# Row maxima of self-attention sent as transfers of 4-byte pieces, and output products in four units instead of two

## The chip, the cores and the metric

The kernel runs on one core of a Trainium2 chip. The metric is the device time of one execution in microseconds. The median of three runs of the kernel before is 3796.76 us.

## The reference

Four blocks in a row work on x of shape (4, 1024, 256), with a condition vector and 77 context rows per batch. L0 is a mixture of experts with a gate, L1 and L2 are transformer blocks (self-attention, cross-attention with the context, MLP), L3 is a cross-attention. The change touches the two self-attentions, which are (L1, in short; L2 has an adaptive normalisation and a gate `g_sa` on the result):

```python
h = layernorm(x, ln1_g, ln1_b)
q, k, v = heads(h @ wq + bq), heads(h @ wk + bk), heads(h @ wv + bv)   # 16 heads of 16
scores = einsum("bqhd,bkhd->bhqk", q, k) / 4                           # 1024 x 1024 per head
x = x + einsum("bhqk,bkhd->bqhd", softmax(scores), v) @ wo + bo + t_sa
```

## The kernel before

After the experts (L0) the program goes four times, once per batch, through one list of steps, `PASS`, written by `pass_schedule`. Every engine walks through the same list and issues what of each step is its own, so the list sets the order on all engines. Modules follow each other in it: L1sa, L1ca, L1mlp, L2sa, L2ca, L2mlp, L3ca; a step's first name is its module.

In a self-attention the 1024 tokens are 8 blocks of 128; `n` is one half of the queries (512, four blocks `t`), `g` one of four groups of four heads. A block of work is a pair (g, n), 8 per module. The softmax's maximum of each query must be known before the exponentials, and goes into the products themselves: q and k of a pair of heads are stacked in the rows of `qs` and `ks`, and row MAXROW of `qs` holds minus the maximum, beside a row of ones in `ks`. So there are two kinds of score products:

- step `A` (g, n, t, j): queries of block t as weights, all keys moving, into two PSUM banks (`ps<-ks,qs` in the trace). VectorE takes the negated maximum of each half of the keys (line 1721, `mxh`).
- step `both` (g, n): VectorE takes the minimum of the halves for all 4 blocks and 4 heads, 128x16 (line 1730, `mx`).
- step `M` (g, n): TensorE transposes `mx` (line 1069) into 16 rows of 128, ScalarE copies them to `mrow` (line 1390), and SyncE sends four transfers, each of 4 rows of 512 bytes, to row MAXROW of `qs` (`stack_maxima`, line 635).
- step `S` (g, n, kt, j): keys of block kt as weights, 512 queries moving (`ps<-qs,ks`). The first of a block waits for its transfers (`maxima_stacked`). ScalarE takes the exponential (line 1406, `probs`).
- steps `PV` (and `PVh`, its first half where score products for maxima are left): probabilities times v (`ps<-probs,v`), summed over kt. `O` copies the sum, `OT` (line 1122) turns it back to tokens, VectorE divides by the sum of exponentials.
- step `aT` turns the result of a half once more, `o` (t2) multiplies two blocks of 128 tokens by `wo` (`ps<-slot,hT` with 256 columns), VectorE adds to x (line 1687, in L2sa after a product with the gate, line 1682) and takes the statistics of the next normalisation, GpSimd the root (line 1768), and `N` (n) normalises the four token blocks of a half (line 1456, `tok`) for the next module. `T` (n) transposes them (line 983).

`self_attention` writes the order: all A, `both` and M in the list `maxima`, the S and PV in `units` of one (g, n, kt); `more` takes from `maxima` so that about two A go with each unit, and they end some 12 units before the last. Block (g, n)'s maxima are taken while an earlier block's units run. `turn` holds `both` and M of a block that is done: `both` comes before the next block's first A, M after its fourth (after the first for block (0, 0)). Near the end, behind unit `end - 6` come the two `aT` of the first half of the tokens, then o(0), o(1) and N(0) of the module that follows, one unit apart. PSUM banks of these steps are given out by `shared`, which takes the one asked for longest ago: A takes (0, 1) or (2, 3), the others (4 to 6) while A are left, and all seven afterwards; bank 7 is PV's. `mx` and `mxh` have two buffers each, used in turn by the blocks.

Of the kernel before, what the change touches and what calls it, by code (L numbers as in the profile page):

```python
# [25 lines left out]
F32 = mybir.dt.float32  # L26
# [6 lines left out]
P = 128  # L33
# [3 lines left out]
HALF = 512  # L37
# [82 lines left out]
def pass_schedule():  # L120
# [9 lines left out]
    def put(tag, *which):  # L130
        steps.extend((tag,) + w for w in which)
# [10 lines left out]
    def self_attention(tag, follow):  # L142
        maxima, turn = [], []
        for g in range(GROUPS):
            for n in range(NH):
                scores = [("A", g, n, t, j) for t in range(TPH) for j in range(GH)]

                behind = 1 if (g, n) == (0, 1) else 4
                maxima += turn[:1] + scores[:behind] + turn[1:] + scores[behind:]
                turn = [("both", g, n), ("M", g, n)]  # L150
        maxima += turn

# [26 lines left out]
        for u in range(end + lag):  # L179
# [23 lines left out]
            if u == end - 6:  # L203
                put(tag, *[("aT", 0, c) for c in range(KC)])
            elif u in (end - 5, end - 4):
                put(tag, ("o", u - end + 5))
            elif u == end - 3:
                put(follow, ("N", 0))
# [82 lines left out]
PASS = pass_schedule()  # L291
HALVED = {k for k in PASS if k[1] == "PVh"}

# [53 lines left out]
def build(nc, T, M):  # L347
    ctx = ExitStack()
    with ctx:
# [220 lines left out]
        def _(sp):  # L570
# [33 lines left out]
            for it in M.passes("blocks"):  # L604
# [18 lines left out]
                def stack_maxima(tag):  # L623

                    for g, n in [(g, n) for g in range(GROUPS) for n in range(NH)] if KIND[tag] == "self" else [(0, 0), (0, 1)]:
                        z, w, _, step = maxima_of(tag, g, n)
                        sp.wait_ge(act_done, upto(act_done, (tag,) + step))
                        if KIND[tag] == "cross":
                            for e in range(2):
                                sp.dma_start(qs[stacked(e, MAXROW, MAXROW + 1), 2 * g:2 * g + w // 2, n * HALF:(n + 1) * HALF].bitcast(F32),  # L630
                                             mrow[e:w:2, z * HALF:(z + 1) * HALF]
                                             ).then_inc(maxima_stacked[g][n], M.add(maxima_stacked[g][n], (tag, e), LOADED))
                        else:
                            for j in range(GH):
                                sp.dma_start(qs[stacked(j % 2, MAXROW, MAXROW + 1), 2 * g + j // 2, n * HALF:(n + 1) * HALF].bitcast(F32),
                                             mrow[TPH * j:TPH * (j + 1), z * HALF:z * HALF + P]
                                             ).then_inc(maxima_stacked[g][n], M.add(maxima_stacked[g][n], (tag, j - GH + 2), LOADED))
# [34 lines left out]
        def _(pe):  # L672
# [238 lines left out]
            for it in M.passes("blocks"):  # L911
# [9 lines left out]
                for name in PASS:  # L921
# [135 lines left out]
                    elif kind == "M":  # L1057
# [4 lines left out]
                        pe.wait_ge(act_done, upto(act_done, *act_was))  # L1062
                        last = (tag, "A", GROUPS - 1, n, TPH - 1, 0) if cross else (tag, "both", g, n)
                        pe.wait_ge(dve_done, upto(dve_done, last, *dve_was))
# [67 lines left out]
                    elif kind == "up":  # L1132
# [9 lines left out]
                        for i, (w, h) in enumerate(products):  # L1142
                            ins = mm(ps[:, b, :], w, h, i == 0, i == len(products) - 1)
                    elif kind == "o":

                        t2 = step[1]
                        a, banks = small()
                        _, act_was, dve_was = take(name, dve=(tag, "x", t2), banks=banks)
                        if KIND[tag] == "mlp":
# [7 lines left out]
                        pe.wait_ge(dve_done, upto(dve_done, *dve_was))  # L1157
                        for i in range(2):
                            t = 2 * t2 + i
# [6 lines left out]
                            else:  # L1166
                                for k in range(KC):
                                    ins = mm(ps[:, a, i * D:(i + 1) * D], hT[:, k, t * P:(t + 1) * P], wo[:, k, :], k == 0, k == KC - 1)
                    ins.then_inc(mm_done, M.add(mm_done, name))


        @block.scalar
        def _(act):
# [143 lines left out]
            for it in M.passes("blocks"):  # L1317
# [3 lines left out]
                for name in PASS:  # L1321
# [61 lines left out]
                    elif kind == "M":  # L1383
                        g, n = step[1:]
                        z, w, _, _ = maxima_of(tag, g, n)
                        act.wait_ge(mm_done, upto(mm_done, name))
                        if not cross and NH * g + n >= 2:
                            act.wait_ge(maxima_stacked[g - 1][n], upto(maxima_stacked[g - 1][n], (tag, 1)))
                        k, m = (w, HALF) if cross else (TPH * GH, P)
# [47 lines left out]
        def _(dve):  # L1437
# [198 lines left out]
            for it in M.passes("blocks"):  # L1636
# [4 lines left out]
                for name in PASS:  # L1641
# [81 lines left out]
                    elif kind == "both":  # L1723

                        g, n = step[1:]
                        z = maxima_of(tag, g, n)[0]
                        if NH * g + n >= 2:
                            dve.wait_ge(mm_done, upto(mm_done, (tag, "M", g - 1, n)))
                        dve.wait_ge(dve_done, upto(dve_done, (tag, "A", g, n, TPH - 1, GH - 1)))
                        dve.tensor_tensor(mx[:, z, 0, :].rearrange("p (c e t) -> p t c e", t=TPH, e=2), mxh[:, z, :, :, 0, :], mxh[:, z, :, :, 1, :], ALU.min  # L1730
                                          ).then_inc(dve_done, M.add(dve_done, (tag, "both", g, n)))
                    elif kind == "O" and by_dve(*name):
# [178 lines left out]
```

## Time and profile before

| | |
|---|---|
| median of 3 runs | 3796.76 us (3792.34 to 3797.68) |
| the profiled execution's own time | 3797.3 us |
| its span, first to last instruction | 3795.5 us |
| TensorE (PE) busy | 91% of the span |
| VectorE (DVE) busy | 59% |
| ScalarE (ACT) busy | 61% |
| granted TensorE clock, mean | 0.961 of full |
| transfers `qs<-mrow` of self-attention | 256, 2 KB each |
| DMA packets | 73089 |

Times in the rows below are microseconds from the span's start; L635 is line 635 of the kernel. "Idle before" in square brackets is how long the engine stood before the instruction, and what ended that. Matmuls are pipelined, so the distance between the starts of two of them tells more than their length. PE has a second row of its own for weight loads (PEld); SPq is the queue of SyncE.

### The profile page before, as it was taken

How to read it: one execution, taken by the hardware profiler on the slowest of the kernel's cores; microseconds unless marked ns; L12 is line 12 of the kernel's file. 1: busy time of each engine (PE TensorE's matmuls, PEld its weight loads, DVE VectorE, ACT ScalarE, POOL GpSimd, SP SyncE). 2: the span in 40 equal slices, each digit the busy share in tenths (PEclk: the TensorE clock that was granted, in tenths of full speed). 3: DMA queues.
4: the chain of work that ended last, by engine and by line, in shares of the span. 5: the costliest groups of instructions: out<-in, count | busy, mean ns of one | idle time of the engine just before them, and what ended most of it. 6: DMA issues, size and time to landing. Idle time of an engine off the chain costs nothing.

```text
span 3795.5 us, 59346 instructions
## 1 busy us (share of the span) xinstructions
PE 3443.8 (91%) x22289; PEld 2023.6 (53%) x22289; DVE 2237.3 (59%) x3533; ACT 2316.6 (61%) x4047; POOL 830.5 (22%) x546
## 2 busy tenths in 40 slices
PE   8999998898999888998898889988998899899988
PEld 6777776434644564446435744465446443564465
DVE  3323324885386556953885559636955487549654
ACT  2333333786577645875786557765874578657764
POOL 0322323003400521024003410051014100340051
PEclk8989989999999999999999999999999999999999
DMA  5001002000000001001000010000000100000000
GB/s 173 7 29 34 6 31 89 1 13 24 27 2 1 13 15 53 2 24 38 2 2 13 12 56 2 24 24 16 2 13 12 56 1 13 24 27 2 7 18 13
DMA packets 73089, 87.17 MB, mean 23 GB/s; under 512 B 11823, under 2 KB 62578, under 8 KB 72694
## 3 DMA queue, kind: packets, MB, share of 16 engines
q1 hardware_dynamic: 47846, 63.23, 5.1%
q10 hardware_dynamic: 24976, 20.15, 1.7%
q8 instruction: 195, 3.19, 0.4%
q14 instruction: 72, 0.59, 0.1%
HBM read 72.49 MB, written 9.56 MB: 22 GB/s over the span
## 4 chain that ended last, share of the span: by engine, by line
PE 76%; DVE 13%; ACT 7%; issue 2%; POOL 1%; DMA 0%; SPq 0%; ACTq 0%; DVEq 0%; POOLq 0%
PE ps L677 71%; DVE mxh L1721 4%; ACT probs L1406 3%; PE ps L1122 3%; DVE ctxk L1670 2%; DVE ow L1746 1%; PE ps L983 1%; DVE tok L1456 1%; DVE x L1687 1%; DVE small L1440 1%; DVE mx L1718 1%; ACT qs L1373 1%; POOL hidl L1832 1%; POOL small L1768 1%; ACT ow L1412 1%
## 5 line engine op out<-in xcount | busy, mean ns | idle before, releaser
L1406 ACT ACTIVATE probs<-ps 128x512 f32<-128x512 f32 (+1 forms) x2176 | 1216.5, 638 | 290.3 <-PE ps L677 247.7
L1721 DVE TENSOR_REDUCE mxh<-ps 128x2 f32<-128x1024 f32 x1024 | 1212.7, 1220 | 155.8 <-PE ps L677 152.7
L677 PE MATMUL ps<-probs,v 128*32 128x256 f32 (+2 forms) x7616 | 727.9, 454 | 6.3 <-ACT probs L1406 6.3
L677 PE MATMUL ps<-ks,qs 64*128 64x512 f32 x2048 | 483.1, 480 | 63.7 <-DVE mxh L1721 45.3
L1768 POOL TENSOR_TENSOR small<-small 128x4 f32<-128x4 f32 x66 | 67.8, 1027 | 2012.8 <-DVE small L1450 2012.8
L677 PE MATMUL ps<-qs,ks 64*128 64x512 f32 x2048 | 455.6, 425 | 4.0 <-DVE mxh L1721 2.5
L677 PEld LDWEIGHTS ps<-ks,qs 64*128 64x128 f32 x2048 | 192.8, 183 | 424.8 <-issue 302.0
L677 PEld LDWEIGHTS ps<-qs,ks 64*128 64x128 f32 x2048 | 248.1, 186 | 184.1 <-ACT probs L1406 150.1
L677 PEld LDWEIGHTS ps<-probs,v 128*32 128x32 f32 (+1 forms) x7616 | 150.2, 108 | 275.8 <-ACT probs L1406 204.6
L677 PE MATMUL ps<-hT,slot 128*128 128x512 f32 x448 | 233.5, 654 | 21.8 <-issue 8.5
L1718 DVE TENSOR_REDUCE mx<-ps 128x4 f32<-128x312 f32 x384 | 166.2, 478 | 146.2 <-PE ps L677 142.8
L1373 ACT ACTIVATE qs<-ps,cols 128x512 fp32r<-128x512 f32 x288 | 180.2, 687 | 101.5 <-PE ps L677 101.0
L677 PE MATMUL ps<-slot,hT 128*128 128x256 f32 x896 | 217.2, 387 | 9.3 <-ACT hT L1417 9.3
L1798 POOL TENSOR_TENSOR hidl<-hid,hidh 128x512 fp32r<-128x512 f32 x96 | 125.6, 1311 | 357.1 <-ACT hid L1282 357.1
L1687 DVE TENSOR_TENSOR x<-x,ps 128x512 f32<-128x512 f32 x80 | 55.0, 687 | 237.6 <-PE ps L677 237.6
L677 PEld LDWEIGHTS ps<-slot,hT 128*128 128x128 f32 x896 | 163.4, 190 | 58.2 <-issue 23.8
L1279 ACT ACTIVATE hidh<-ps,cols 128x512 fp32r<-128x512 f32 x96 | 66.1, 688 | 162.6 <-PE ps L677 162.4
L1832 POOL TENSOR_TENSOR hidl<-hid,hidh 128x512 fp32r<-128x512 f32 x128 | 161.7, 1300 | 7.2 <-ACT hid L1424 5.8
L1850 POOL TENSOR_TENSOR ql<-whole,qh 128x512 fp32r<-128x512 f32 x80 | 101.8, 1273 | 279.5 <-ACT whole L1358 279.5
L1122 PE MATMUL ps<-ident,ow 128*128 128x128 f32 x640 | 101.8, 282 | 60.6 <-DVE ow L1746 31.7
L983 PE MATMUL ps<-ident,tok 128*128 128x128 f32 x448 | 77.1, 311 | 80.3 <-DVE tok L1456 62.3
L677 PEld LDWEIGHTS ps<-hT,slot 128*128 128x128 f32 x448 | 85.5, 206 | 116.5 <-issue 90.5
(221 smaller groups left out, 5919.2 us busy)
## 6 DMA issues: line engine op xcount, KB each, us to landing
slot<-in_L_w SPq DMA_DIRECT2D x8, 1024.0 KB, 10.0
slot<-in_L_fc_w SPq DMA_DIRECT2D x8, 1024.0 KB, 5.4
xin<-in_x ACTq DMA_DIRECT2D x5, 1024.0 KB, 6.1
x_after_block<-x ACTq DMA_DIRECT2D x20, 256.0 KB, 2.4
xin<-x_after_block SPq DMA_DIRECT2D x5, 1024.0 KB, 5.5
ew<-in_L_e_w SPq DMA_DIRECT2D x6, 768.0 KB, 14.3
x<-in_x ACTq DMA_DIRECT2D x4, 1024.0 KB, 6.9
qs<-mrow SPq DMA_DIRECT2D x256, 2.0 KB
```

The costliest lines, as they stand in the source:

```text
L677: return pe.matmul(out, lhsT, rhs, start=start, stop=stop)
L983: ins = pe.transpose(ps[:, b, i * P:(i + 1) * P], tok[:, t, c * P:(c + 1) * P], ident[:])
L1122: ins = pe.transpose(ps[:, a, i * P:(i + 1) * P], ow[:, o:o + P], ident[:])
L1373: ins = act.activation(qs[:, pair, n * HALF:(n + 1) * HALF], ps[:, b, :], ACT.Identity, bias=qs_rows)
L1406: ins = act.activation(dst, src, ACT.Exp, scale=SCALE)
L1687: dve.tensor_tensor(xx, xx, src, ALU.add).then_inc(dve_done, M.add(dve_done, (tag, "x", t2)))
L1718: dve.tensor_reduce(mx[:, z, t, j0:j0 + GH], ps[:, a, 0:GH * SP_].rearrange("p (j s) -> p j s", s=SP_), AX.X, ALU.max, negate=True).then_i ...
L1721: dve.tensor_reduce(mxh[:, z, t, j // 2, j % 2, :], ps[:, a:a + 2, :], AX.X, ALU.max, negate=True).then_inc(dve_done, M.add(dve_done, name))
L1768: pool.tensor_tensor(rstd[:, tt], ve[:, tt], nhalf[:, tt], ALU.pow).then_inc(pool_done, M.add(pool_done, (tag, "rstd", h)))
L1798: pool.tensor_tensor(hidl0[:, (E * n + e) % 2, m % 4, :], hid0[:, m % 4, :], hidh0[:, (E * n + e) % 2, m % 4, :].bitcast(F32), ALU.subtrac ...
L1832: pool.tensor_tensor(hidl[:, n, m, :], hid[:, n, m, :], hidh[:, n, m, :].bitcast(F32), ALU.subtract).then_inc(pool_done, M.add(pool_done, ...
L1850: pool.tensor_tensor(lo[:, c, part], whole[:, whole_of(name)[0], 0:kn], hi[:, c, part].bitcast(F32), ALU.subtract).then_inc(pool_done, M.a ...
```

## The change

Blocks other than (0, 0) have no step M any more. `both` is now a step of each 128 queries, (g, n, t), 128x4, and stands behind the first A of the next t. As soon as it is done SyncE sends, for each of the four heads, one column of `mx` (128 partitions of one number, 4 bytes each) to 128 numbers in row MAXROW of `qs`: 16 transfers per block instead of four. The wait of a block's first S is for all 16. Block (0, 0) keeps its transposition and its four transfers, behind the minimum of its last t.

The output products of the first half are cut: `oh` (t2) multiplies the first 128 tokens, `o` (t2) the second into the same bank. The four stand behind the units `end - 5` to `end - 2`, and N(0) of the next module behind `end - 1`, two units later than before.

```diff
     def self_attention(tag, follow):
-        maxima, turn = [], []
+        maxima, last = [], []
         for g in range(GROUPS):
             for n in range(NH):
-                scores = [("A", g, n, t, j) for t in range(TPH) for j in range(GH)]
-
-                behind = 1 if (g, n) == (0, 1) else 4
-                maxima += turn[:1] + scores[:behind] + turn[1:] + scores[behind:]
-                turn = [("both", g, n), ("M", g, n)]
-        maxima += turn
+                for t in range(TPH):
+                    maxima += [("A", g, n, t, 0)] + last + [("A", g, n, t, j) for j in range(1, GH)]
+                    last = [("both", g, n, t)]
+                if (g, n) == (0, 0):
+                    maxima += last
+                    last = [("M", g, n)]
+        maxima += last
...
-            elif u in (end - 5, end - 4):
-                put(tag, ("o", u - end + 5))
-            elif u == end - 3:
+            elif u in (end - 5, end - 3):
+                put(tag, ("oh", (u - end + 5) // 2))
+            elif u in (end - 4, end - 2):
+                put(tag, ("o", (u - end + 4) // 2))
+            elif u == end - 1:
                 put(follow, ("N", 0))
...
                         z, w, _, step = maxima_of(tag, g, n)
+                        if KIND[tag] == "self" and (g, n) != (0, 0):
+                            for t in range(TPH):
+                                sp.wait_ge(dve_done, upto(dve_done, (tag, "both", g, n, t)))
+                                at_column = n * HALF + t * P
+                                for j in range(GH):
+                                    sp.dma_start(qs[stacked(j % 2, MAXROW, MAXROW + 1), 2 * g + j // 2, at_column:at_column + P].bitcast(F32),
+                                                 mx[:, z, 0, TPH * j + t:TPH * j + t + 1]
+                                                 ).then_inc(maxima_stacked[g][n], M.add(maxima_stacked[g][n], (tag, j - GH + 2) if t == TPH - 1 else None, LOADED))
+                            continue
                         sp.wait_ge(act_done, upto(act_done, (tag,) + step))
...
-                        for i in range(2):
+                        for i in (0,) if kind == "oh" else (1,) if in_two else range(2):
                             t = 2 * t2 + i
...
                     elif kind == "both":
 
-                        g, n = step[1:]
+                        g, n, t = step[1:]
                         z = maxima_of(tag, g, n)[0]
-                        if NH * g + n >= 2:
-                            dve.wait_ge(mm_done, upto(mm_done, (tag, "M", g - 1, n)))
-                        dve.wait_ge(dve_done, upto(dve_done, (tag, "A", g, n, TPH - 1, GH - 1)))
-                        dve.tensor_tensor(mx[:, z, 0, :].rearrange("p (c e t) -> p t c e", t=TPH, e=2), mxh[:, z, :, :, 0, :], mxh[:, z, :, :, 1, :], ALU.min
-                                          ).then_inc(dve_done, M.add(dve_done, (tag, "both", g, n)))
+                        if (g, n) == (1, 0):
+                            dve.wait_ge(mm_done, upto(mm_done, (tag, "M", 0, 0)))
+                        elif NH * g + n > 2 and t == 0:
+                            dve.wait_ge(maxima_stacked[g - 1][n], upto(maxima_stacked[g - 1][n], (tag, 1)))
+                        dve.wait_ge(dve_done, upto(dve_done, (tag, "A", g, n, t, GH - 1)))
+                        dve.tensor_tensor(mx[:, z, 0, :].rearrange("p (c e t) -> p t c e", t=TPH, e=2)[:, t], mxh[:, z, t, :, 0, :], mxh[:, z, t, :, 1, :], ALU.min
+                                          ).then_inc(dve_done, M.add(dve_done, (tag, "both", g, n, t)))
```

ScalarE's wait in step M for the transfers of two blocks ago goes too, since `mrow` is written once per module.

VectorE in the steady stretch of L1sa, from one division by the sums (`rc`, `tok`) to the next, before:

```order
L1756 RECIPROCAL rc<-ps 128x16
L1758 TENSOR_TENSOR tok<-ps,rc 128x4x64
L1721 TENSOR_REDUCE mxh<-ps 128x2 x4
L1730 TENSOR_TENSOR mx<-mxh 128x4x4
L1721 TENSOR_REDUCE mxh<-ps 128x2 x12
L1756 RECIPROCAL rc<-ps 128x16
L1758 TENSOR_TENSOR tok<-ps,rc 128x4x64
```

and now:

```order
L1774 RECIPROCAL rc<-ps 128x16
L1776 TENSOR_TENSOR tok<-ps,rc 128x4x64
L1737 TENSOR_REDUCE mxh<-ps 128x2
L1748 TENSOR_TENSOR mx<-mxh 128x4
L1737 TENSOR_REDUCE mxh<-ps 128x2 x4
L1748 TENSOR_TENSOR mx<-mxh 128x4
L1737 TENSOR_REDUCE mxh<-ps 128x2 x4
L1748 TENSOR_TENSOR mx<-mxh 128x4
L1737 TENSOR_REDUCE mxh<-ps 128x2 x4
L1748 TENSOR_TENSOR mx<-mxh 128x4
L1737 TENSOR_REDUCE mxh<-ps 128x2 x3
L1774 RECIPROCAL rc<-ps 128x16
```

Sixteen reductions stand there in both; one minimum of 128x16 has become four of 128x4, each behind the first reduction of the following t.

TensorE in L1sa around the end of the maxima, where the last M stood, before:

```order
L677 MATMUL ps<-probs,v 32x256 x4
L677 MATMUL ps<-ks,qs 128x512 x2
L1069 MATMUL ps<-ident,mx 16x128
L677 MATMUL ps<-qs,ks 128x512 x2
L677 MATMUL ps<-probs,v 32x512 x4
```

and now:

```order
L689 MATMUL ps<-probs,v 32x256 x4
L689 MATMUL ps<-ks,qs 128x512 x2
L689 MATMUL ps<-qs,ks 128x512 x2
L689 MATMUL ps<-probs,v 32x512 x4
```

The score products for the exponentials follow the last one for the maxima directly.

TensorE in L1sa from o(0) (`slot_99,hT`) to the transposition T(0) of L1ca (`ident,tok`), before:

```order
L677 MATMUL ps<-slot_99,hT 128x256 x4
L677 MATMUL ps<-qs,ks 128x512 x2
L677 MATMUL ps<-probs,v 32x512 x4
L677 MATMUL ps<-qs,ks 128x512 x2
L677 MATMUL ps<-slot_99,hT 128x256 x4
L677 MATMUL ps<-qs,ks 128x512 x2
L677 MATMUL ps<-probs,v 32x512 x4
L677 MATMUL ps<-qs,ks 128x512 x4
L677 MATMUL ps<-probs,v 32x512 x4
L677 MATMUL ps<-qs,ks 128x512 x4
L677 MATMUL ps<-probs,v 32x512 x4
```

and now, from the first half of o(1) on:

```order
L689 MATMUL ps<-slot_99,hT 128x256 x2
L689 MATMUL ps<-qs,ks 128x512 x2
L689 MATMUL ps<-probs,v 32x512 x4
L689 MATMUL ps<-qs,ks 128x512 x2
L689 MATMUL ps<-slot_99,hT 128x256 x2
L689 MATMUL ps<-qs,ks 128x512 x2
L689 MATMUL ps<-probs,v 32x512 x4
L689 MATMUL ps<-qs,ks 128x512 x2
L689 MATMUL ps<-probs,v 32x512 x8
L995 MATMUL ps<-ident,tok 128x128 x8
```

Behind the last output product now stand one unit's PV and S, the last PV, and T(0) (`ident,tok`); before, the S of two more units stood between.

## Rows read from the trace of the kernel before

**Rows 1.** The page: busy time of the engines, and the chain that ended last.
```profile
PE 3443.8 (91%) x22289; PEld 2023.6 (53%) x22289; DVE 2237.3 (59%) x3533; ACT 2316.6 (61%) x4047; POOL 830.5 (22%) x546
...
PE 76%; DVE 13%; ACT 7%; issue 2%; POOL 1%; DMA 0%; SPq 0%; ACTq 0%; DVEq 0%; POOLq 0%
```

**Rows 2.** Timeline, TensorE, steady stretch: start, us, line, operation, [idle before <-ended by].
```profile
738.57 0.50 PE L677 MATMUL ps<-ks,qs 64*128 64x512 f32 x2
739.00 0.28 PE L1069 MATMUL ps<-ident,mx 128*16 128x128 f32 x1
...
740.24 0.50 PE L677 MATMUL ps<-ks,qs 64*128 64x512 f32 x2
740.57 0.40 PE L677 MATMUL ps<-qs,ks 64*128 64x512 f32 x2
...
741.47 0.50 PE L677 MATMUL ps<-ks,qs 64*128 64x512 f32 x2
...
750.04 0.66 PE L1122 MATMUL ps<-ident,ow 128*128 128x128 f32 x4 [0.43 <-ACT ow L1412]
...
771.45 0.66 PE L1122 MATMUL ps<-ident,ow 128*128 128x128 f32 x4 [0.43 <-ACT ow L1412]
```

**Rows 3.** Timeline, VectorE, the same stretch.
```profile
757.12 0.19 DVE L1730 TENSOR_TENSOR mx<-mxh 128x16 f32<-128x16 f32 x1
757.22 4.61 DVE L1721 TENSOR_REDUCE mxh<-ps 128x2 f32<-128x1024 f32 x4
```

**Rows 4.** Timeline, end of the maxima of the first L1sa.
```profile
840.64 0.50 PE L677 MATMUL ps<-ks,qs 64*128 64x512 f32 x2
842.72 0.19 DVE L1730 TENSOR_TENSOR mx<-mxh 128x16 f32<-128x16 f32 x1
...
843.06 0.27 PE L1069 MATMUL ps<-ident,mx 128*16 128x128 f32 x1 [1.92 <-DVE mx L1730]
...
843.25 0.52 PE L677 MATMUL ps<-qs,ks 64*128 64x512 f32 x2
...
849.67 0.73 PE L677 MATMUL ps<-qs,ks 64*128 64x512 f32 x4
```

**Rows 5.** Windows between two copies of the sum: us, busy by engine, granted clock, DMA.
```profile
834.98:872.97 37.99, 34.86 (x234) 13.14 (x233) 14.34 (x30) 29.27 (x59) 1.02 (x1) 1.00 0.09 29
...
2763.05:2803.61 40.56, 37.39 (x235) 13.56 (x233) 15.72 (x32) 29.37 (x60) 1.02 (x1) 0.92 0.01 1
...
sum 314.48, PE 289.28 PEld 106.96 DVE 120.25 ACT 234.33 POOL 8.14; mean PE 36.16 PEld 13.37 DVE 15.03 ACT 29.29 POOL 1.02
```

**Rows 6.** Timeline, VectorE, in the lead of the first L1sa.
```profile
679.88 9.23 DVE L1721 TENSOR_REDUCE mxh<-ps 128x2 f32<-128x1024 f32 x8 [0.34 <-PE ps L677]
```

**Rows 7.** Timeline, SyncE's queue and TensorE, block (0, 0)'s transfers.
```profile
690.08 2.54 SPq L635 DMA_DIRECT2D qs<-mrow  x4
...
693.71 0.57 PE L677 MATMUL ps<-qs,ks 64*128 64x512 f32 x2 [0.60 <-DMA qs<-mrow]
```

**Rows 8.** DMA issues: count, KB each, us from issue to landing.
```profile
ident<-in_ident SPq DMA_DIRECT2D x1, 64.0 KB, 2.3
```

**Rows 9.** One tile (`cond`): duration ns min/median/max, first and last start.
```profile
L1180 ACTq DMA_DIRECT2D cond<-in_condT x9: 486/487/700, 1.9 to 3011.3; - x9
```

**Rows 10.** Timeline, end of the first L1sa.
```profile
864.82 0.50 PE L677 MATMUL ps<-qs,ks 64*128 64x512 f32 x2
...
868.16 1.38 DVE L1456 TENSOR_SCALAR tok<-x,small 128x256 f32<-128x256 f32 x4 [1.13 <-POOL small L1768]
...
871.84 1.07 PE L677 MATMUL ps<-probs,v 128*32 128x512 f32 x8 [0.78 <-ACT probs L1406]
```

**Rows 11.** Timeline, end of the first L2sa.
```profile
1216.53 0.51 PE L677 MATMUL ps<-qs,ks 64*128 64x512 f32 x2
...
1217.36 0.69 DVE L1687 TENSOR_TENSOR x<-x,tok 128x512 f32<-128x512 f32 x1
...
1220.59 1.38 DVE L1456 TENSOR_SCALAR tok<-x,small 128x256 f32<-128x256 f32 x4 [1.13 <-POOL small L1768]
```

More of the change, by code:

```diff
@@ L291 @@
 PASS = pass_schedule()
-HALVED = {k for k in PASS if k[1] == "PVh"}
+HALVED = {k for k in PASS if k[1] in ("PVh", "oh")}
 def by_dve(tag, kind, *step):
@@ L1062, in _ @@
                         pe.wait_ge(act_done, upto(act_done, *act_was))
-                        last = (tag, "A", GROUPS - 1, n, TPH - 1, 0) if cross else (tag, "both", g, n)
+                        last = (tag, "A", GROUPS - 1, n, TPH - 1, 0) if cross else (tag, "both", g, n, TPH - 1)
                         pe.wait_ge(dve_done, upto(dve_done, last, *dve_was))
@@ L1143, in _ @@
                             ins = mm(ps[:, b, :], w, h, i == 0, i == len(products) - 1)
-                    elif kind == "o":
+                    elif kind in ("oh", "o"):
                         t2 = step[1]
-                        a, banks = small()
-                        _, act_was, dve_was = take(name, dve=(tag, "x", t2), banks=banks)
+                        in_two = (tag, "oh", t2) in HALVED
+                        if kind == "oh" or not in_two:
+                            a, banks = small()
+                            _, act_was, dve_was = take((tag, "o", t2), dve=(tag, "x", t2), banks=banks)
+                        else:
+                            a, act_was, dve_was = M.where(name), [], []
                         if KIND[tag] == "mlp":
@@ L1168, in _ @@
                                     ins = mm(ps[:, a, i * D:(i + 1) * D], hT[:, k, t * P:(t + 1) * P], wo[:, k, :], k == 0, k == KC - 1)
+                        if kind == "oh":
+                            continue
                     ins.then_inc(mm_done, M.add(mm_done, name))
@@ L1386, in _ @@
                         act.wait_ge(mm_done, upto(mm_done, name))
-                        if not cross and NH * g + n >= 2:
-                            act.wait_ge(maxima_stacked[g - 1][n], upto(maxima_stacked[g - 1][n], (tag, 1)))
                         k, m = (w, HALF) if cross else (TPH * GH, P)
```

## The prediction

> **What bounds the kernel now.** The page's totals and its chain of waits come first: TensorE is busy for 91% of the span and carries 76% of the chain that ended last [rows 1]. Half a microsecond won on TensorE is therefore won for the kernel wherever TensorE runs without a gap, and nothing is won beside it. The change touches the two self-attention modules (L1sa, L2sa), run for each of 4 batches: 8 passes.
>
> The timeline of TensorE in a steady stretch shows such a pass [rows 2]. Score products for the maxima (`ks,qs`, step A) start every 1.23 us (740.24 to 741.47) without idle time. Where the transposition of the maxima (step M, L1069) stands between two of them, the step is 1.67 us (738.57 to 740.24). From one output transposition to the next (750.04 to 771.45), one block of four heads and 512 queries, 21.41 us pass. VectorE is close behind but not the bound: with work waiting it makes four reductions in 4.61 us, so (4.61 - 1.22)/3 = 1.13 us each, against TensorE's 1.23 [rows 3]. The small minimum (`both`, L1730) lasts 0.19 us, but the next reduction starts 0.10 us after it [rows 3].
>
> At the end of the maxima the cost is another [rows 4]: after the last score product (840.64) TensorE idles 1.92 us for the last minimum before it can transpose, and its next product starts at 843.25, 2.61 us after the last A instead of the 0.33 us between 740.24 and 740.57 [rows 2]. In six of the eight passes more follows: the stretch that holds this idle time is 37.99 us long with the full clock, but up to 40.56 us with a granted clock of 0.92, that is, part of it at 1.2 GHz instead of 2.4; the eight stretches add up to 314.48 us [rows 5].
>
> **What the change removes.** Of 8 transpositions M per pass 7 go, with 7 ScalarE copies and 28 transfers. Six stand in the steady stretch: 1.67 - 1.23 = 0.44 us each, 6 x 8 x 0.44 = **21.1 us**. I take all of it, because TensorE has no gap there and neither VectorE (1.13 against 1.23) nor ScalarE waits behind it. The seventh stands at the end of the maxima: 2.61 - 0.33 = 2.28 us, times 8 = **18.2 us**. The S products that follow need nothing of VectorE. With the idle time the clock drop behind it should go too: 314.48 - 8 x 37.99 = **10.6 us**. Its bounds are 0 (the drops only move) and 10.6. I take 10.6, since two passes with the same idle time and no drop bear out what the stretch takes at full clock.
>
> **What it adds on VectorE.** 32 minima of 128x4 instead of 8 of 128x16 per pass, 24 more. Each costs the queue 0.10 us by the start of the reduction behind it [rows 3]; the bounds are 0 and the whole 0.19 us. In the steady stretch TensorE's 1.23 leaves 0.10 us per reduction, 0.40 us per four, for one minimum: hidden. The minimum is queued behind the next reduction, whose end it need not wait for, and a second pair of banks holds the product meanwhile. In the lead it is not hidden: eight reductions from 679.88 follow each other in 9.23 us without a gap, so VectorE is the bound there [rows 6]. Two new minima fall into that run: 2 x 0.10 x 8 = **1.6 us lost** (0 to 3 x 0.19 x 8 = 4.6).
>
> **What it adds on SyncE and the DMA engines.** 16 transfers per block instead of 4, each of 128 pieces of 4 bytes: 7 x 16 - 28 = 84 more per pass. They hold up nobody but step S of their block, and behind them on SyncE stand only loads that wait for the end of the maxima anyway. Two prices are unknown, issue and landing. Issue: four of today's (4 pieces each) take 2.54 us, 0.64 each [rows 7], and a load of 128 pieces of 8 bytes takes 0.487 us [rows 9]. Landing: a load of 128 pieces of 512 bytes with little ahead of it lands 2.3 us after its issue [rows 8]; from the start of the fourth issue of today's (690.08 + 3 x 0.64 = 692.0) to TensorE's start at 693.71 are 1.7 us [rows 7]. So the last minimum of a block is followed by 3 x 0.64 + 2.3, and 0.1 to react, 4.3 us (lower bound 3 x 0.49 + 1.7 = 3.2). What is available: in the steady stretch S of a block follows 8 A products after the first of the next block, 7 x 1.23 + 0.33 = 8.9 us, less some 2.3 us (two reductions of 1.13) until VectorE has made the minimum: 6.6 us. At block (3,1) it is tighter: the minimum starts at 842.72 and lasts 0.19, the new minima ahead of it may push its end to 843.0, and S(3,1,0,0), the third of the four `qs,ks` products from 849.67, starts at about 850.0 and will start 2.28 us earlier: 847.7 - 843.0 = 4.7 us [rows 4]. **Cost 0**, with 0.4 us to spare there, which rival 2 weighs. Sixteen issues of 0.64 are 10.2 us of a block of 21; what dearer ones would do is rival 1.
>
> The rows of 128 pieces are loads from memory; none goes from 128 partitions into one. The Trainium skill (DMA: Bandwidth & Descriptors, Rules for kernel authors) speaks against the change: it says to coalesce many small transfers into a large one, and that a strided last dimension becomes one descriptor per element and should be rearranged. No row here shows such a transfer. By that rule the time would come out on the other side, which is the first rival below.
>
> **The output products.** Steps o(0) and o(1), 1.99 us each today, become four of half that in the next four units, and the normalisation N(0) moves from behind unit 61 to behind unit 63. TensorE's work is the same. Gained: today TensorE waits 0.78 us for the last exponentials [rows 10], because they were bunched behind the two long products; with four short ones I leave 0.15, so 0.63 gained per pass. Lost: the transposition T(0) of the next module comes sooner after the last output product. From the end of o(1) (864.82) TensorE has 0.43 + 1.00 + 0.42 + 1.00 + 1.00 + 0.15 = 4.0 us of work, and T(0)'s first four transpositions would be done at 4.5. The normalised rows are there at 868.16 + 1.38 - 864.82 = 4.72 us [rows 10], and the fourth transposition ends at about 4.9: 0.4 lost. In L2sa a product with the gate comes first: 1220.59 + 1.38 - 1216.53 = 5.44, so 1.1 lost [rows 11]. There the bank of o(0) is also wanted by an S product 1.43 us after it, while VectorE lets go of it at 1217.36 + 0.69 - 1216.53 = 1.52 [rows 11]: 0.15 more. Per pass +0.2 in L1sa and -0.65 in L2sa, together 4 x 0.45 = **1.8 us lost** (bounds: 8 x 0.63 = 5.0 gained, 4 x 3 = 12 lost if the wait costs the clock again).
>
> **The sum.** 21.1 + 18.2 + 10.6 - 1.6 - 1.8 = 46.5 us. The profiled execution took 3797.3 us (span 3795.5), 0.5 above the median of the three runs, 3796.8; against that median the forecast is 3796.8 - 46.5 = **3750.3 us**, 1.2% faster. This kernel can be told from no change at about 0.2%, 7.6 us.
>
> **The rivals.**
> 1. *SyncE and its small transfers become the bound* (slower). Place: step S of every block. Sixteen transfers must go out in the 21.0 us that a block lasts without its transposition, so it decides from 21.0/16 = 1.31 us per transfer, and the kernel as a whole is slower from about 1.37: 16 x 1.37 - 21.0 = 0.9 us per block, times 48 blocks, is 44 us. At 1.5 us it would be 3 x 48 = 144 us, 3894 us. For it: no row has 4-byte pieces into one partition. Against it: 0.487 us for the nearest piece count [rows 9]. Chance 0.07.
> 2. *The last block's transfers land late* (4.3 us grows past 4.7). At 6 us 1.3 us are lost in each pass, 10.4 in all: 3761 us. Chance 0.11.
> 3. *The clock gives nothing back*, because the drops move, or because L2sa's wait before T(0) brings one: 3750.3 + 10.6 = 3761 us, up to 3769 with drops of 2 us at four of them. Chance 0.12.
> 4. *VectorE takes over the steady stretch*: 24 x 8 x 0.19 = 36 us lost of 46.5, 3787 us. Against it is its 0.10 us of slack per reduction. Chance 0.03.
> 5. *The transpositions were hidden*, so that only o's shift is seen: 3797 us. The step of 1.67 us speaks against it. Chance 0.02.
>
> **How the numbers follow.** The forecast has 0.65. Its own range runs from 3741 (all gains, T(0) not waiting: 46.5 + 1.6 + 6.8 = 54.9 gained) to 3759 (minima at 4.6, so 3.0 more, and both waits before T(0) twice as long, so 4 x 1.5 = 6.0 more). Rivals 2 and 3 reach to 3769. The range 3740 to 3770 leaves out rivals 1, 4 and 5 and some of the tails, about 0.18. Faster by over 0.2%: 0.65 + 0.11 + 0.12 + 0.02 = 0.90; within 0.2%: 0.03; slower: 0.07.
>
> **What would show it.** Right: the step from one output transposition to the next falls from 21.41 to 21.0; TensorE no longer waits for the minimum at the end of the maxima; the eight stretches last about 35.1 us (37.99 - 2.28 - 0.63) with a clock of 1.00; packets grow by about 896 x 128 = 115,000; a TensorE wait of 0.4 us (L1sa) and 1.1 us (L2sa) stands before T(0). Wrong: waits of TensorE for `qs<-mx`, an issue over 1.3 us, a granted clock below 1 behind the wait for T(0), or TensorE waits for reductions in the steady stretch.

## The result, and the profile after

The changed kernel takes 3807.47 us (median of 13 runs, 3795.10 to 3816.78) against 3792.44 us for the kernel before, measured beside it; the ratio is 1.0044, 95% interval 1.0031 to 1.0058, without one of the 13 executions of the kernel before that took 6517.69 us. It is **slower by 0.44%, some 17 us**, where 46.5 us faster were forecast.

The profiled execution of the changed kernel (3795.1 us) is the fastest of its 13, and a plain comparison of the two spans (3793.3 against 3795.5 us) misleads. The self-attention's first score product stands at 649.30 us in it and at 665.67 before: 16.4 us won in the experts, whose code is untouched. In the profiles of this study that product stands at 649 to 652 us or at 660 to 666 us, with the changed maxima and without them: the experts vary between executions (why is not shown), and that variation is in every ratio below. So I compare the passes by stage, and for the experiments I also give the time from that first score product to the end of the span: 3129.8 us before, 3144.0 after, **14.2 us more**. First the page of the changed kernel:

```profile
PE 3426.3 (90%) x22233; PEld 2018.0 (53%) x22233; DVE 2286.4 (60%) x3725; ACT 2306.2 (61%) x3991; POOL 831.2 (22%) x546
...
PE 77%; DVE 13%; ACT 6%; issue 2%; POOL 1%; DMA 1%; SPq 0%; ACTq 0%; DVEq 0%; POOLq 0%
...
qs<-mx SPq DMA_DIRECT2D x896, 0.5 KB, 2.0
```

Against [rows 1] TensorE is busy 17.5 us less, yet the median time is not less. Windows show where the time goes. These are the eight leads, from the first score product to the first output transposition (columns: window, length, busy time of PE, PEld, DVE, ACT and POOL, granted clock, DMA share, GB/s). Before:

```profile
665.67:728.63 62.96, 55.16 (x328) 26.66 (x328) 51.40 (x47) 41.74 (x74) 8.36 (x4) 1.00 0.00 1
...
sum 504.91, PE 443.21 PEld 213.78 DVE 411.19 ACT 329.92 POOL 66.97; mean PE 55.40 PEld 26.72 DVE 51.40 ACT 41.24 POOL 8.37
```

And after:

```profile
649.30:718.91 69.61, 57.65 (x327) 28.31 (x327) 56.43 (x55) 41.57 (x73) 8.33 (x4) 0.95 0.03 1
...
sum 552.60, PE 458.50 PEld 224.49 DVE 451.71 ACT 328.16 POOL 66.65; mean PE 57.31 PEld 28.06 DVE 56.46 ACT 41.02 POOL 8.33
```

**The leads have grown by 47.7 us**, with VectorE busy 40.5 us longer and the granted clock at 0.95 in all eight. The steady stretches behind them (first to last output transposition but the tail's) sum, before and then after:

```profile
sum 856.27, PE 839.06 PEld 354.23 DVE 792.30 ACT 716.95 POOL 0.00; mean PE 104.88 PEld 44.28 DVE 99.04 ACT 89.62 POOL 0.00
```

```profile
sum 839.37, PE 822.50 PEld 349.65 DVE 794.15 ACT 706.28 POOL 0.00; mean PE 102.81 PEld 43.71 DVE 99.27 ACT 88.29 POOL 0.00
```

16.9 us less. The ends of the maxima, from the last score product for maxima to the step `aT`, before and then after:

```profile
2768.70:2786.87 18.17, 16.21 (x95) 4.75 (x91) 3.55 (x6) 13.08 (x28) 0.00 (x0) 0.81 0.01 1
...
sum 135.31, PE 119.83 PEld 36.51 DVE 28.32 ACT 103.91 POOL 0.00; mean PE 14.98 PEld 4.56 DVE 3.54 ACT 12.99 POOL 0.00
```

```profile
2764.10:2778.08 13.98, 13.64 (x94) 4.34 (x91) 3.59 (x6) 12.81 (x27) 0.00 (x0) 1.00 0.04 2
...
sum 111.84, PE 109.15 PEld 34.70 DVE 28.69 ACT 102.43 POOL 0.00; mean PE 13.64 PEld 4.34 DVE 3.59 ACT 12.80 POOL 0.00
```

23.5 us less, with the clock at 1.00 in all eight. What follows up to the output transposition behind T(0) is 8.5 us longer (148.80 against 140.27 us over the eight passes, from `aT`). Together: 47.7 - 16.9 - 23.5 + 8.5 = 15.8 us slower in the self-attentions, where the medians say 17 with an interval of 12 to 22.

The lead's growth has one place. VectorE in the changed kernel, first lead:

```profile
658.21 1.06 DVE L1748 TENSOR_TENSOR mx<-mxh 128x4 f32<-128x4 f32 x1
...
664.65 4.00 DVE L1748 TENSOR_TENSOR mx<-mxh 128x4 f32<-128x4 f32 x1
...
674.63 0.15 DVE L1748 TENSOR_TENSOR mx<-mxh 128x4 f32<-128x4 f32 x1
```

GpSimd in the same stretch:

```profile
657.97 1.28 POOL L1868 TENSOR_TENSOR ql<-whole,qh 128x512 fp32r<-128x512 f32 x1 [3.61 <-ACT whole L1376]
...
664.10 4.53 POOL L1841 TENSOR_TENSOR x<-xin,rows_now 128x2048 f32<-128x2048 f32 x1
```

And TensorE:

```profile
669.93 0.79 PE L689 MATMUL ps<-ks,qs 64*128 64x512 f32 x2 [4.55 <-DVE mxh L1737]
...
683.26 3.46 PE L689 MATMUL ps<-slot,hT 128*128 128x256 f32 x8
```

A minimum of 512 numbers lasts **4.00 us** where others last 0.15. It ends at 668.65 and GpSimd's addition at 668.63; the one of 1.06 us ends at 659.27 and GpSimd's subtraction at 659.25. The pattern repeats in all eight passes (1.06 to 1.07 and 3.99 to 4.01 us): 8 x (3.85 + 0.91) = 38 us of VectorE's 40.5. TensorE stands 4.55 us, and a stretch at half clock begins behind it (its next products of keys and queries last 0.79 us instead of 0.49). A second such stretch follows in the same lead, at 683.26, where eight products with `slot` last 3.46 us instead of the 1.99 of the kernel before. In the kernel before the lead's one minimum comes at 689.14, and GpSimd's addition is over by then, at 685.04:

```profile
680.47 4.57 POOL L1823 TENSOR_TENSOR x<-xin,rows_now 128x2048 f32<-128x2048 f32 x1
```

The Trainium skill (SBUF — State Buffer, Who interferes with whom) has the rule: a VectorE instruction with two inputs in SBUF and a GpSimd instruction that reads SBUF exclude each other, and whichever comes second waits until the first is done. This trace agrees to 0.02 us, twice in each pass. The reductions of PSUM in the lead, beside the same addition, keep their pace: 9.23/8 = 1.15 us [rows 6].

### The profile page after: what moved, and what is told of

Same layout as the page of the kernel before. It is cut to its first block, busy times and chain, and to the rows that moved or that the text cites. A ratio compares the mean times of both kernels' runs of the same rounds, so it can differ in the third digit from the quotient of the medians.

```text
span 3793.3 us, 59978 instructions
## 1 busy us (share of the span) xinstructions
PE 3426.3 (90%) x22233; PEld 2018.0 (53%) x22233; DVE 2286.4 (60%) x3725; ACT 2306.2 (61%) x3991; POOL 831.2 (22%) x546
## 2 busy tenths in 40 slices
DMA packets 200328, 87.28 MB, mean 23 GB/s; under 512 B 139951, under 2 KB 189810, under 8 KB 199926
## 4 chain that ended last, share of the span: by engine, by line
PE 77%; DVE 13%; ACT 6%; issue 2%; POOL 1%; DMA 1%; SPq 0%; ACTq 0%; DVEq 0%; POOLq 0%
PE ps L689 72%; DVE mxh L1737 3%; PE ps L1134 3%; ACT probs L1422 2%; DVE ctxk L1686 2%; DVE ow L1764 1%; PE ps L995 1%; DVE tok L1472 1%; DVE small L1456 1%; ACT qs L1391 1%; DVE x L1703 1%; DVE mx L1748 1%; POOL small L1786 1%; DVE mx L1734 1%; ACT ow L1428 1%
## 5 line engine op out<-in xcount | busy, mean ns | idle before, releaser
L689 PE MATMUL ps<-slot,hT 128*128 128x256 f32 x896 | 227.4, 397 | 9.3 <-ACT hT L1433 9.3
```

The source lines that it names most:

```text
L689: return pe.matmul(out, lhsT, rhs, start=start, stop=stop)
```

## The experiments

Ratios are to the kernel before, measured beside each group of experiments, with their 95% intervals; it took 3787 us beside e1 to e4, 3788 beside e5 to e8 and 3796 beside e9 and e10. "x us faster" is worked out from the ratio. The second figure for each leaves the experts out; it comes from one profiled execution each, from the first score product of self-attention to the end of the span, against the 3129.8 us of before:

| | by the ratio | first score product to end |
|---|---|---|
| e1 | 22 faster | 23.0 faster |
| e2 | 42 faster | 34.4 faster |
| e3 | 28 faster | 39.9 faster |
| e4 | 43 slower | 42.7 slower |
| e5 | 42 faster | 34.8 faster |
| e6 | 53 faster | 43.4 faster |
| e7 | 12 slower | 6.8 slower |
| e8 | 22 faster | 21.2 faster |
| e9 | 33 slower | 51.2 slower |
| e10 | 46 faster | 42.7 faster |

**e1: one minimum for block (0, 0).** Its result is not needed before its transposition, so cutting it buys nothing.

```diff
+                if (g, n) == (0, 1):
+                    last = [("both", 0, 0, TPH - 1), ("M", 0, 0)]
                 for t in range(TPH):
                     maxima += [("A", g, n, t, 0)] + last + [("A", g, n, t, j) for j in range(1, GH)]
-                    last = [("both", g, n, t)]
-                if (g, n) == (0, 0):
-                    maxima += last
-                    last = [("M", g, n)]
+                    last = [("both", g, n, t)] if (g, n) != (0, 0) else []
```

> The changed kernel, but block (0, 0), whose maxima are still transposed, keeps one minimum of 128x16 instead of four of 128x4. In the profile of the changed kernel the minimum of its second 128 queries lasts 4.00 us in each of the 8 passes, and ends with GpSimd's addition x<-xin (4.53 us) beside it; the first lasts 1.06 us. Theory A, a minimum with both inputs in SBUF waits while GpSimd works: the lead loses its 46.8 us over the 8 passes, about 3759 us (3752 to 3768), no minimum over 0.3 us. Rival B, each extra VectorE instruction in the lead costs only its own time: 3 x 8 x 0.15 = 4 us less than the change, about 3803 us. Rival C, the small transfers slow the kernel: no change, 3807 us.

Measured 3766.65 us, ratio 0.9942 (0.9920 to 0.9965). No minimum lasts over 0.3 us, B and C fall, but about 8 us of the expected gain are missing. I had put the minimum behind the next block's first score product, where the kernel before has it ahead; its transposition waits for that reduction too, 1.51 us instead of the 0.44 before, 8.6 us in eight passes:

```profile
674.14 0.27 PE L1080 MATMUL ps<-ident,mx 128*16 128x128 f32 x1 [1.51 <-DVE mx L1748]
```

Four of its eight leads also have a granted clock of 0.95 or 0.97.

**e2: the same four minima with one input.**

```diff
+                        if (g, n) == (0, 0):
+                            dve.tensor_reduce(mx[:, z, 0, :].rearrange("p (c e t) -> p t c e", t=TPH, e=2)[:, t], mxh[:, z, t].rearrange("p c h e -> p c e h"), AX.X, ALU.min
+                                              ).then_inc(dve_done, M.add(dve_done, (tag, "both", g, n, t)))
+                            continue
```

> The changed kernel with its four minima of block (0, 0) in the same places, each made by a TENSOR_REDUCE of the halves (one input) instead of a TENSOR_TENSOR of two. A: if two inputs in SBUF are what waits for GpSimd, these last about 0.15 us beside the addition, and the time is that of the kernel with one minimum plus up to 4 us, 3759 to 3763 us. Rival A2, any VectorE operation on SBUF waits for GpSimd: still 4 us at the second minimum, 3807 us. Rival B: 3807 us.

Measured 3744.71 us, ratio 0.9889 (0.9862 to 0.9915), 14 us below what I had said. Its four runs lie between 3737 and 3759 us, and the profiled one, whose trace I read, is the 3759. In that one the experts take 12 us more than in e1's profile (the first score product stands at 661.47 us against 649.22), and three leads have stretches at half clock; whether the others lack both is not on record. VectorE, then GpSimd:

```profile
670.38 0.15 DVE L1749 TENSOR_REDUCE mx<-mxh 128x4 f32<-128x8 f32 x1
...
676.83 0.15 DVE L1749 TENSOR_REDUCE mx<-mxh 128x4 f32<-128x8 f32 x1
```

```profile
676.28 4.58 POOL L1845 TENSOR_TENSOR x<-xin,rows_now 128x2048 f32<-128x2048 f32 x1
```

The same numbers from SBUF into SBUF, in the middle of the addition, in 0.15 us. A stands, A2 falls. The edit changes the operation together with the number of inputs; a row of the changed kernel tells the two apart, a TENSOR_TENSOR whose one input is in SBUF and the other in PSUM, inside a GpSimd subtraction:

```profile
867.97 1.27 POOL L1868 TENSOR_TENSOR ql<-whole,qh 128x512 fp32r<-128x512 f32 x1 [4.64 <-ACT whole L1376]
```

```profile
868.35 0.69 DVE L1703 TENSOR_TENSOR x<-x,ps 128x512 f32<-128x512 f32 x1 [1.94 <-PE ps L689]
```

It lasts 0.69 us, as it does with GpSimd idle (849.72), and all 80 of them last 0.68 to 0.69. So it is the second input in SBUF.

**e3: the addition later.**

```diff
+                        if KIND[tag] == "self":
+                            pool.wait_ge(dve_done, upto(dve_done, (tag, "both", 0, 0, TPH - 1)))
                         pool.tensor_tensor(x[:], ...
```

> The changed kernel with its four two-input minima, but GpSimd's addition x<-xin of the self-attention waits until the last minimum of block (0, 0). A: the second minimum falls from 4.00 to about 0.15 us; the first keeps its 1.06 us (GpSimd's kl<-whole,kh is still beside it); the time is about 3760 us (3754 to 3772), a few us more if the addition meets the minima of block (0, 1). Rival B or C: 3807 us.

Measured 3759.03 us, ratio 0.9926 (0.9900 to 0.9951). VectorE in the lead:

```profile
661.06 1.06 DVE L1748 TENSOR_TENSOR mx<-mxh 128x4 f32<-128x4 f32 x1
...
667.51 0.16 DVE L1748 TENSOR_TENSOR mx<-mxh 128x4 f32<-128x4 f32 x1
```

The second minimum is short again, the first still waits for GpSimd's subtraction of 1.27 us, as expected. So GpSimd's instruction matters, not the place in VectorE's order.

**e4: the kernel before with only that.** Block (0, 0)'s minimum cut into four; transpositions, transfers and output products as before.

```diff
+                if (g, n) == (0, 0):
+                    scores = [s for t in range(TPH) for s in [("A", g, n, t, 0)] + [("both", g, n, t - 1)] * (t > 0) + [("A", g, n, t, j) for j in range(1, GH)]]
```

> The kernel before with one part of the change alone: block (0, 0)'s minimum cut into four of 128x4, behind the first score product of the next 128 queries, as in the change; everything else (transpositions, transfers, output products) as before. A: the lead's loss is this and nothing else, so about 47 us slower than before, 3839 us (3830 to 3846). Rival B: 4 us slower, 3796 us. Rival C: as before, 3792 us.

Measured 3829.53 us, ratio 1.0114 (1.0090 to 1.0139), 43 us slower. Its leads, as windows:

```profile
649.18:719.95 70.77, 59.10 (x328) 29.05 (x329) 56.38 (x50) 41.71 (x74) 8.32 (x4) 0.93 0.00 1
...
sum 559.11, PE 466.88 PEld 226.28 DVE 450.89 ACT 329.91 POOL 66.55; mean PE 58.36 PEld 28.28 DVE 56.36 ACT 41.24 POOL 8.32
```

54.2 us more than before in the leads, with the clock at 0.93 to 0.95; the steady stretches and the ends of the maxima are as before, and it is 9 us less between the passes, where the granted clock of the longer stretches is 0.94 to 0.95 against 0.92 to 0.93. Three more small instructions per pass cost nearly as much as the whole change was to bring, 46.5 us.

**e5: e1 with the minimum in its old place.**

```diff
+                if (g, n) == (0, 1):
+                    maxima += [("both", 0, 0, TPH - 1)]
+                    last = [("M", 0, 0)]
```

> The changed kernel with one minimum of 128x16 for block (0, 0), this time ahead of the next block's first score product, where the kernel before has it. e1 had it behind that product, and its transposition M waited 1.51 us instead of 0.44 (8 x 1.07 = 8.6 us). Expected: M waits 0.44 us again, the lead is 0.3 us a pass shorter than in the kernel before, and the whole 38 to 43 us faster than before (3745 to 3752 us if before is 3788). If e1's remaining distance to e2 was something else, the time stays at e1's, 20 us below before.

Measured 3746.35 us, ratio 0.9888 (0.9862 to 0.9914), as expected. This is the change without its mistake: 42 us faster.

**e6: e5 with the output products in two units, as before.** The maxima alone are changed.

> As e5, and the output products of the first half in two units as in the kernel before, so the maxima alone are changed. By the prediction's own step the split costs 1.8 us over the 8 passes, so this would be 1.8 us faster than e5; if the shorter wait for the last exponentials is the larger part, it is up to 5 us slower; if the wait before T(0) counts more than I took, up to 12 us faster.

Measured **3738.14 us**, ratio 0.9861 (0.9839 to 0.9883): 53 us faster than before and the best of the study. It is 8.2 us below e5 in the medians and 8.6 us in the profiles without the experts, more than the step's 1.8. In the traces the stretches from `aT` to the output transposition behind T(0) sum to 148.80 us in e5 and 140.20 in e6. The rest of e6 has what the maxima give, as windows: the leads, and then the ends of the maxima:

```profile
sum 500.29, PE 438.09 PEld 212.95 DVE 412.34 ACT 327.90 POOL 66.98; mean PE 54.76 PEld 26.62 DVE 51.54 ACT 40.99 POOL 8.37
```

```profile
sum 111.88, PE 109.18 PEld 34.73 DVE 28.72 ACT 102.45 POOL 0.00; mean PE 13.65 PEld 4.34 DVE 3.59 ACT 12.81 POOL 0.00
```

**e7: the kernel before with the output products in four units.** The edit is the change's own for `oh` and `o`, with `N(0)` behind `end - 1`.

> The kernel before with the output products' part alone: first half in four units, N(0) behind the last unit. By the prediction 1.8 us slower than before, with the wait for the last exponentials down from 0.78 to 0.15 us and a wait before T(0); bounds 5 us faster and 12 us slower. In the changed kernel's trace the distance from the first product behind the maxima to T(0) in the first L1sa is 29.30 us against 29.13, so I look for about 2 to 6 us slower.

Measured 3803.79 us, ratio 1.0031 (1.0015 to 1.0048), 12 us slower; its trace has 8.5 us more from `aT` on (148.78 against 140.27 us): 0.54 in a pass of L1sa and 1.60 in one of L2sa. TensorE at the end of the first L2sa:

```profile
1215.64 0.59 PE L679 MATMUL ps<-qs,ks 64*128 64x512 f32 x2 [0.18 <-ACT probs L1414]
1216.15 1.13 PE L679 MATMUL ps<-slot,hT 128*128 128x256 f32 x4
...
1221.80 0.59 PE L679 MATMUL ps<-qs,ks 64*128 64x512 f32 x2 [0.17 <-ACT probs L1414]
1222.32 2.19 PE L679 MATMUL ps<-probs,v 128*32 128x512 f32 x16
1224.75 1.64 PE L985 MATMUL ps<-ident,tok 128*128 128x128 f32 x8 [0.24 <-DVE tok L1464]
1226.23 0.60 PE L1124 MATMUL ps<-ident,ow 128*128 128x128 f32 x4
```

The wait before T(0) is 0.24 us, less than I had taken. But from T(0)'s first transposition to the next step's pass 1.48 us where it was 0.93 (1224.55 to 1225.48 in the kernel before), because the normalised rows `tok` arrive one by one (VectorE writes the four from 1224.19 to 1225.57), and score products wait twice, 0.18 and 0.17 us, for a bank that ScalarE still reads. One half of an output product (the row of x4) costs 1.06 us from start to next start, more than half of the 1.92 of the whole (x8).

**e8: the kernel before with the new way for block (3, 1) alone.** Seven blocks keep their transposition.

> The kernel before with the new way for the last block (3, 1) alone: its four minima of 128x4 and 16 transfers of 4-byte pieces; the other seven blocks keep their transposition. This separates the idle time at the end of the maxima and the clock behind it from the steady stretch. Expected: the steady step stays 21.41 us, TensorE's wait of 1.92 us is gone, no granted clock below 1 between it and T(0) in any pass; 23 to 29 us faster than before. If the clock drops only move, 12 to 18 us.

Measured 3771.00 us, ratio 0.9943 (0.9921 to 0.9964), 22 us faster. Two of the stretches of [rows 5] in it, the second being the one that was 40.56 us long:

```profile
829.70:866.08 36.38, 34.82 (x235) 13.16 (x232) 14.38 (x31) 29.11 (x58) 1.02 (x1) 1.00 0.12 30
2740.73:2777.10 36.37, 34.81 (x235) 13.14 (x232) 15.77 (x33) 29.11 (x58) 1.02 (x1) 1.00 0.03 1
```

All eight sum to 291.01 us, 23.5 below the 314.48 of before: 1.6 us each for the idle time and 10.6 for the clock, and the drops do not come back before T(0).

**e9: twice as many small transfers.** As e5, each of 64 pieces instead of 128.

```diff
                                 for j in range(GH):
-                                    sp.dma_start(qs[stacked(j % 2, MAXROW, MAXROW + 1), 2 * g + j // 2, at_column:at_column + P].bitcast(F32),
...
+                                    for part in range(2):
+                                        sp.dma_start(qs[stacked(j % 2, MAXROW, MAXROW + 1), 2 * g + j // 2, at_column + 64 * part:at_column + 64 * part + 64].bitcast(F32),
+                                                     mx[64 * part:64 * part + 64, z, 0, TPH * j + t:TPH * j + t + 1]
...
```

> As e5, but each of the small transfers cut in two: 32 per block, of 64 pieces of 4 bytes, 1792 in all. It tells how far SyncE and the small transfers are from being the bound (rival 1). In the changed kernel's trace one issue takes 0.60 us in the median and lands in 2.0 us. If an issue's price does not depend on its number of pieces: 32 x 0.6 = 19.2 us of SyncE in a block of 21.0, so the steady stretch still holds at 21.0, but the last block's transfers come later than its first score products and TensorE waits there: up to 10 us slower than e5. If the price goes with the pieces (0.3 us each): as e5. If it is above 0.66 us with two per head: the blocks get longer, 1 us or more each, over 50 us.

Measured 3825.54 us, ratio 1.0086 (1.0063 to 1.0109), 33 us slower than before where e5 is 42 faster. SyncE's queue runs without a pause through the steady stretch, and TensorE waits for it at the end of the maxima:

```profile
715.97 84.34 SPq L636 DMA_DIRECT2D qs<-mx  x125
```

```profile
837.95 0.57 PE L690 MATMUL ps<-qs,ks 64*128 64x512 f32 x2 [2.86 <-DMA qs<-mx]
```

84.34/125 = 0.67 us per transfer of 64 pieces, and 32 of them, 21.6 us, do not fit into a block of 21.0: the third case of the expectation. An issue costs nearly the same with half the pieces (0.597 us in the median against 0.601), so with 16 transfers, 10.7 us at that rate, the change has nearly a factor of two in hand.

**e10: no transposition at all.** As e6, block (0, 0) too by small transfers, all minima by one-input reductions.

> As e6 (maxima alone, output products in two), and block (0, 0) has no transposition either: its maxima go by 16 small transfers too, and all minima are one-input TENSOR_REDUCE, which e2 showed not to wait for GpSimd. From the last minimum of block (0, 0) to the first score product of the exponentials there are 4.57 us in the kernel before (689.14 to 693.71); now 0.15 + 3 x 0.6 + 2.0 + 0.1 = 4.1 us, and TensorE is spared M (0.3 us). Expected: 0 to 1 us less per pass, so 0 to 8 us faster than e6 (3730 to 3738 us if before is 3788). If the transfers of the earlier 128 queries queue up, or land later than in the steady stretch, the same as e6 or up to 8 us slower.

Measured 3746.90 us, ratio 0.9880 (0.9858 to 0.9902). The intervals of e6 and e10 overlap, and without the experts the profiles differ by 0.7 us; no gain is shown. TensorE still waits for block (0, 0)'s row, now for `qs<-mx`:

```profile
677.29 0.86 PE L687 MATMUL ps<-qs,ks 64*128 64x512 f32 x2 [0.67 <-DMA qs<-mx]
```

Five of its eight leads last 62.2 to 62.8 us at full clock, some 0.1 us less than e6's on average, but three have a granted clock of 0.97 and last 63.6 to 64.0.

## Why the prediction was wrong

**The step that failed** is "What it adds on VectorE", its second half: "Two new minima fall into that run: 2 x 0.10 x 8 = 1.6 us lost (0 to 3 x 0.19 x 8 = 4.6)". The leads grew by 47.7 us although one of their two transpositions was gone; against e6, which has one minimum there, they are 552.60 - 500.29 = **52.3 us** longer. By itself the cut cost 43 us (e4). Two things were wrong in it. The price of 0.19 us came from rows where GpSimd is idle [rows 3, 4] (it is busy for 0.00 us in all windows of the steady stretch and of the end of the maxima), and I took it as an upper bound for a place where GpSimd works on SBUF for 4.5 us; neither the forecast nor a rival looked at GpSimd's timeline in the lead, although the change moves instructions of VectorE past it. And I took VectorE's extra time as the loss, where half clock came with TensorE's wait (0.93 to 0.95 granted in all sixteen leads of the change and of e4): of the 54 us in e4's leads only 38 are longer minima. All five rivals had other places; the 0.07 for slower stood on SyncE, which was not it, so even that chance was not for this mechanism.

The other terms, each by its own number:

- **Steady transpositions, 21.1 us: right.** The step between output transpositions fell from 21.41 to 20.98 us. The stages hold 16.9 us for five of the six, and the lead of e6 has 4.6 us less, of which 1.6 is a clock drop that one lead of before had: 16.9 + 3.0 = 19.9, with the loss by the minima in the lead already in it. (The lead is 0.38 us a pass shorter, so the further minima, of the other blocks, cost it next to nothing where GpSimd lets them through.)
- **The end of the maxima, 18.2 us: mis-sized.** It gave 1.61 us a pass, 12.9 in all, instead of 2.28. S starts 0.34 us behind the last A, as forecast, but its second product waits for a bank that VectorE is still reducing, so the pair takes 1.12 us to the next step (829.11 to 830.23) instead of the 0.46 before (843.25 to 843.71):

```profile
829.83 0.46 PE L689 MATMUL ps<-qs,ks 64*128 64x512 f32 x1 [0.34 <-DVE mxh L1737]
```

- **The clock behind it, 10.6 us: right,** 23.5 - 12.9 = 10.6, shown in isolation by e8. Rival 3's first half falls. But the change opened a new place for such drops, the lead.
- **Transfers, 0 us: right.** No TensorE wait for `qs<-mx` in the changed kernel. Issue was taken as 0.64 us and is 0.60 to 0.67, landing as 2.3 us and is 2.0. The Trainium skill's rule on many small transfers (DMA: Bandwidth & Descriptors, Rules for kernel authors), and with it rival 1, did not decide: packets rose from 73089 to 200328 and the steady stretch got shorter. (That is 142 packets per new transfer where the forecast of 115,000 has 128; why is not shown.) e9 shows that the rule does bite at twice the count, for between 64 and 128 pieces the price is per transfer. Rival 2's late landing was not seen either, and rivals 4 and 5 fall with the step of 20.98 us.
- **Output products, 1.8 us lost: mis-sized.** 8.5 us in the traces, 12 (6 to 18) in e7. The wait for the last exponentials fell from 0.78 to 0.17 us as forecast; but I called TensorE's work the same, and it is not: two pairs of score products with something between them take 0.43 us each (849.61 to 850.04 in the changed kernel) against 0.66 for both in a row (866.25 to 866.91 before), and short runs of output products cost 0.1 us each. T(0) takes 1.29 us instead of 0.93 in L1sa too (859.53 to 860.82, before 872.84 to 873.77); with two units' pairs separated (2 x 0.2 us), four short runs (4 x 0.1), T(0)'s 0.36 and the 0.61 gained at the last exponentials that is 0.4 + 0.4 + 0.36 - 0.61 = 0.55 us; 0.54 is measured. In L2sa T(0) is slower still and the waits before it and for a bank come on top.

With 52.3 in place of 1.6 (in the 47.7 the gain of the lead's transposition, part of the 21.1, is already taken off), 12.9 in place of 18.2 and 8.5 in place of 1.8, the same sum gives 21.1 + 12.9 + 10.6 - 52.3 - 8.5 = -16.2, a slowdown, as measured. Without the minima of block (0, 0) it gives 36 us faster; e5 measures 42 (33 to 52), and 34.8 in its profile without the experts. Without the split as well it gives 44.6; e6 measures 53 (44 to 61), and 43.4 without the experts.

## What to carry to other kernels

Before an instruction of VectorE is moved or cut into several, look at what GpSimd does at the new place, not only at the old: a VectorE operation with two SBUF inputs may there wait for the whole of a GpSimd instruction, and its duration in a quiet row is no bound. Give it one input, or leave it where GpSimd is quiet; and change only what needs the change, for block (0, 0) gained nothing by being cut. Where a wait is added to an engine that paces TensorE, price the clock with it, and when a step is split, count again what its neighbours cost in smaller groups.

## What the runs showed of the hardware that I had not expected

- A TENSOR_TENSOR of 128x4 with both inputs in SBUF took 4.00 us beside GpSimd's addition of 128x2048 (4.53 us), ending 0.02 us after it; a TENSOR_REDUCE of 128x8 from SBUF in the same place took 0.15 us.
- With a wait of 4.55 us on TensorE the granted clock was 0.95 in all eight leads. With the wait gone it is 1.00 in all eight in e6, but three leads of e2 and one of e3 are longer than their others by 2.6 to 4.3 us at a granted clock of 0.92 to 0.95, and leads at 0.95 to 0.97 stand in e1 (four), e5 (two), e10 (three) and the kernel before (one), so the wait is not the only thing that brings it.
- A transfer of 64 pieces of 4 bytes cost SyncE's queue 0.597 us in the median (e9), one of 128 pieces 0.601 (the changed kernel).
- A TENSOR_TENSOR of 128x512 with one input in SBUF and one in PSUM took its usual 0.69 us inside a GpSimd subtraction of 1.27 us.
